# Four small probability-times-value units and a 32-row key matrix in a fused two-attention kernel

## The chip, the cores and the metric

One core of a Trainium2 chip. The time is that of one execution on the device, in microseconds (us). The median of three runs of the kernel before is 1574.19 us (1571.65 to 1574.8).

## What is computed

```python
# x (16, 100, 128), ctx_768 (16, 1444, 96): a Flamingo-like block, float32
x = x + tanh(g_xattn[0]) * xattn(layernorm(x), ctx_768, ...)     # 16 heads of 64, 1444 keys
x = x + tanh(g_ffn[0]) * ffn(layernorm(x), ...)
# ffn(X): per batch of 100 tokens, 16 heads of 8 (the "small attention"), then a mixture of 8 experts
h = rmsnorm(X, norm1_w)
q, k, v = (h @ wq), (h @ wk), (h @ wv)          # each (b, 100, 16, 8)
scores = einsum('bshd,bthd->bhst', q, k) / sqrt(8)
attn = softmax(scores)
ctx = einsum('bhst,bthd->bshd', attn, v)
X = X + ctx @ wo
...                                              # router, top 2 of 8 experts, shared expert
```

## The kernel before

Everything is written by hand, engine by engine, with semaphores. The main loop runs over the 16 batches; batch 0 ("first") and batch 15 ("last") are written out, and the other 14 are a hardware loop whose body holds an odd and an even batch. One turn here means one batch. The score matrix of the large attention (1444 keys x 1600 rows of head and token) is worked through in 24 units a batch: 12 chunks of the keys (eleven of 128 and one of 36) for each half of the heads. In unit i PE issues `score_unit` (L728 to L732: six products of 400 columns, f16 in high and low parts), then `pv_unit` for the unit two before (L747: again six products). ACT takes each unit's scores through two exponentials (L951, L952), and `probs_rest` (L431) makes the low half `p_lo`, on DVE or, for the units in `LO_POOL`, on POOL. PV products of unit i need the `p_lo` of unit i - 2. Chunk 11 of each half has 36 keys: its scores are 36 columns wide (unit 11), its PV products have 36 contraction rows (unit 13).

All else of a batch is cut into small aux units, which `plan` puts into the 24 units by hand; `steps` splits each unit's list in three: after the scores, between the first pair of PV products and the other four (`middle`), and at the end. Each aux unit writes one of two PSUM banks in turn, and PE waits before a unit until the one before the last is out of its bank (`last` in `run_aux`). The kinds: `t` and `q` transposes and query products for the next batch, `p` a product whose row maximum DVE takes (L813 on PE, L1247 on DVE; the planner spreads 39 of them by `LOAD` and `F_LOAD`, expected DVE loads), `y0`/`y1` the output of the large attention (L840, L1265, L1269), and `f`, the small attention of the batch before. Its units, in order, with the main unit i in which each is put:

- f0 (8) transposes the normalized tokens; f1 (9) makes q, k and v (L847 to L849). DVE copies `qT` and `v9` and builds `kbd` (L1276): the key matrix copied for all 16 heads, zero outside a head's 8 rows, 128 x 1600.
- f2 to f5 (10, 11, 12, 13) are the scores of four heads each: one product of `qT` with 400 columns of `kbd` over 128 rows (L853; an f32 product shows as two records). DVE takes the maxima and subtracts them (L1281, L1282), ACT the exponential (L961).
- f6 to f9 (12, 13, 14, 15) transpose the probabilities (L858); ACT copies them out to `pT` (L999).
- f10 (16) is probability times value, 16 heads in a row (L862: weights 100x100, 9 columns), and DVE divides (L1286, L1287). f11, f12 (18, 19) transpose and multiply by wo; f13 (23) is the transpose for the experts.

So with k the third of a unit: unit 14 has f8, one `p`, two `p`; unit 15 has `y0`, then f9 and a `p`, then two `p`; unit 16 `y0`, f10, `p`; unit 17 `y0`, a `p`, two `p`. Behind the last batch the same small attention runs once more among the first experts (`LAST`, with expert units `e` between). Three functions carry the order of PE: `run_aux`, `aux` and the loop body.

## Time and profile before

| | us |
|---|---|
| median of three runs | 1574.19 |
| span of the profiled execution, first to last instruction | 1570.3 |
| what lies around it, against that median | 3.9 |

The page's slices of the span, in 40 equal parts, digits in tenths; PEclk is the granted TensorE clock:

```profile
PE   5789999999999999999998999999999999888898
DVE  2787767766776767676766777667767685765765
PEclk9599999999999999999999999999999999899999
```

A view of the trace names an instruction by its line, engine, output and inputs, and the shape (partitions x elements). For PE, 97*128 is the contraction rows and the output rows of the product; x2 says that two records were merged. A duration of merged records is from the first start to the last end, and an end of PE is modelled, so starts are the safer reading. In brackets stands how long the engine sat idle before it, and what ended that.

### The profile page before, as it was taken

Reading aid. Unit: us, or ns where it says so; the run is one execution under the profiler, and the core shown is the slowest. Engines: PE = TensorE matmul, PEld = TensorE weight load, DVE = VectorE, ACT = ScalarE, POOL = GpSimd, SP = SyncE. Lnnn points to the kernel's source line nnn. Section 1 sums busy time; section 2 is a strip of 40 time slices with the busy share of each in tenths; the row PEclk is TensorE's granted clock in tenths of the full one; section 3 lists DMA queues with packets and bytes.
Section 4 is the critical chain, followed back from the end, with each engine's and each line's share of the span. In section 5 each row is a group of like instructions: output and inputs, shape, how many; then the busy total and the mean of one; then the engine's idle time right before and its main releaser. Section 6 shows DMA issues by size and latency. Waiting matters only on the chain.

```text
span 1570.3 us, 29033 instructions
## 1 busy us (share of the span) xinstructions
PE 1432.2 (91%) x8968; PEld 849.7 (54%) x8968; DVE 1085.7 (69%) x1948; ACT 832.3 (53%) x1236; POOL 561.2 (36%) x705
## 2 busy tenths in 40 slices
PE   5789999999999999999998999999999999888898
PEld 4245555555555555555555555555555645555676
DVE  2787767766776767676766777667767685765765
ACT  2145656565656555555545565656555554454554
POOL 3023333333333333243333343333333243444554
PEclk9599999999999999999999999999999999899999
DMA  7000000000000000000000000000000000000000
GB/s 195 0 15 1 15 1 16 1 17 1 15 1 16 1 5 11 2 16 1 15 1 16 1 15 1 16 1 15 1 13 4 1 1 1 1 1 1 7 7 11
DMA packets 14994, 18.08 MB, mean 12 GB/s; under 512 B 3046, under 2 KB 12490, under 8 KB 14858
## 3 DMA queue, kind: packets, MB, share of 16 engines
q1 hardware_dynamic: 14858, 16.26, 3.6%
q8 instruction: 86, 1.41, 0.4%
q14 instruction: 50, 0.41, 0.1%
HBM read 15.38 MB, written 0.82 MB: 10 GB/s over the span
## 4 chain that ended last, share of the span: by engine, by line
PE 59%; DVE 17%; issue 9%; ACT 6%; POOL 5%; DMA 1%; DVEq 1%; POOLq 0%; ACTq 0%; SPq 0%
PE psum L747 13%; PE psum L728 7%; PE psum L813 6%; PE psum L732 6%; PE psum L730 6%; DVE mx L1247 4%; PE psum L840 4%; PE psum L760 3%; PE psum L862 3%; ACT p_hi L952 3%; PE psum L853 3%; PE psum L773 2%; DVE p_lo L431 2%; DVE kbd L1276 2%; POOL p_lo L431 2%
## 5 line engine op out<-in xcount | busy, mean ns | idle before, releaser
L951 ACT ACTIVATE p<-psum 128x800 f32<-128x800 f32 (+1 forms) x384 | 321.3, 837 | 564.1 <-PE psum L732 558.2
L1247 DVE TENSOR_REDUCE mx<-psum 128x1 f32<-128x512 f32 (+3 forms) x624 | 387.2, 652 | 63.5 <-PE psum L813 58.5
L431 POOL TENSOR_TENSOR p_lo<-p,p_hi 128x800 f16<-128x800 f32 x128 | 236.3, 1847 | 472.9 <-ACT p_hi L952 461.2
L952 ACT ACTIVATE p_hi<-psum 128x800 f16<-128x800 f32 (+1 forms) x384 | 318.8, 830 | 0.0
L431 DVE TENSOR_TENSOR p_lo<-p,p_hi 128x800 f16<-128x800 f32 (+1 forms) x256 | 269.2, 1051 | 54.5 <-ACT p_hi L952 25.5
L813 PE MATMUL psum<-cT_hi,qk_hi 96*128 96x512 f16 (+3 forms) x624 | 236.2, 389 | 47.2 <-DVE mx L1247 15.0
L747 PE MATMUL psum<-p_hi,c_hi 128*128 128x400 f16 (+1 forms) x768 | 197.4, 338 | 21.3 <-POOL p_lo L431 14.7
L728 PE MATMUL psum<-qk_hi,cT_hi 97*128 97x400 f16 (+1 forms) x768 | 198.3, 340 | 11.7 <-ACT p_hi L952 5.5
L730 PE MATMUL psum<-qk_lo,cT_hi 96*128 96x400 f16 (+1 forms) x768 | 198.0, 339 | 0.0
L732 PE MATMUL psum<-qk_hi,cT_lo 96*128 96x400 f16 (+1 forms) x768 | 197.3, 339 | 0.0
L747 PE MATMUL psum<-p_lo,c_hi 128*128 128x400 f16 (+1 forms) x768 | 195.9, 336 | 0.0
L747 PE MATMUL psum<-p_hi,c_lo 128*128 128x400 f16 (+1 forms) x768 | 195.0, 336 | 0.0
L813 PEld LDWEIGHTS psum<-cT_hi,qk_hi 96*128 96x128 f16 (+1 forms) x624 | 61.2, 98 | 175.5 <-DVE mx L1247 71.9
L566 POOL TENSOR_TENSOR y_sum<-y_sum,y_sb 100x128 f32<-100x128 f32 x192 | 107.9, 562 | 55.3 <-DVE y_sb L1269 32.9
L556 POOL TENSOR_TENSOR c_lo<-ctx_nat,c_hi 128x1056 f16<-128x1056 f32 (+1 forms) x32 | 40.1, 1273 | 234.9 <-ACT c_hi L940 234.9
L747 PEld LDWEIGHTS psum<-p_hi,c_hi 128*128 128x128 f16 (+1 forms) x768 | 70.6, 100 | 80.2 <-issue 26.4
L730 PEld LDWEIGHTS psum<-qk_lo,cT_hi 96*128 96x128 f16 (+1 forms) x768 | 76.0, 99 | 58.5 <-issue 4.2
L732 PEld LDWEIGHTS psum<-qk_hi,cT_lo 96*128 96x128 f16 (+1 forms) x768 | 75.2, 98 | 59.4 <-issue 5.1
L747 PEld LDWEIGHTS psum<-p_hi,c_lo 128*128 128x128 f16 (+1 forms) x768 | 74.8, 97 | 57.5 <-issue 2.7
L728 PEld LDWEIGHTS psum<-qk_hi,cT_hi 97*128 97x128 f16 (+1 forms) x768 | 68.7, 99 | 63.6 <-issue 30.8
L747 PEld LDWEIGHTS psum<-p_lo,c_hi 128*128 128x128 f16 (+1 forms) x768 | 72.3, 101 | 50.6 <-issue 13.2
L621 POOL TENSOR_TENSOR p_lo<-p,p_hi 128x400 f16<-128x400 f32 x72 | 67.7, 945 | 73.6 <-ACT p_hi L966 73.3
(189 smaller groups left out, 1952.4 us busy)
## 6 DMA issues: line engine op xcount, KB each, us to landing
ctx_nat<-in_ctx_dram SPq DMA_DIRECT2D x16, 528.0 KB
wg<-in_L_ffn_e_gate_dram SPq DMA_DIRECT2D x1, 1024.0 KB, 5.5
wu<-in_L_ffn_e_up_dram SPq DMA_DIRECT2D x1, 1024.0 KB, 7.8
wd<-in_L_ffn_e_down_dram SPq DMA_DIRECT2D x8, 128.0 KB, 5.7
out_dram<-sqb SPq DMA_DIRECT2D x4, 200.0 KB
x<-in_x_dram SPq DMA_DIRECT2D x1, 600.0 KB
p<-in_L_xattn_w_q_dram SPq DMA_DIRECT2D x1, 512.0 KB, 4.2
wd_hi<-in_L_xattn_w_o_dram SPq DMA_DIRECT2D x1, 512.0 KB
```

The costliest lines, as they stand in the source:

```text
L431: engine.tensor_tensor(p_lo[0:m, i % 3, :, :], p32[0:m, i % 3, :, :], p_hi[0:m, i % 3, :, :], ALU.subtract).then_inc(lo_made(b, i)[0], 1)
L566: g.tensor_tensor(to, x, y, ALU.add).then_inc(y_add, 1)
L621: g.tensor_tensor(hid_lo[:, n % HS, :], hidden[:, n % 3, :], hid_hi[:, n % HS, :], ALU.subtract).then_inc(hid_lo_out, 1)
L728: mm(outs[k], cT_hi[parity][:, cols], qk_hi[parity][:, qs[k]], start=True, stop=False)
L730: mm(outs[k], cT_hi[parity][0:C, cols], qk_lo[parity][:, qs[k]], start=False, stop=False)
L732: t = mm(outs[k], cT_lo[parity][:, cols], qk_hi[parity][0:C, qs[k]], start=False, stop=True)
L747: t = mm(outs[k], w[parity][0:m, j, :], p[0:m, i % 3, k, :], start=(j == 0 and w is c_hi and p is p_hi), stop=(j == CH - 1 and w is c_lo))
L813: t = mm(bank[0:r, 0:w], qk_hi[parity][0:C, rt * P:rt * P + r], cT_hi[parity][0:C, part * MW:part * MW + w], start=True, stop=True)
L840: t = mm(bank[0:S, k * YW:(k + 1) * YW], acc_sb[half][:, h // 4, (h % 4) * S:(h % 4 + 1) * S], Nh[:, half * HALF + h, :], start=True, stop ...
L951: a(p32[0:m, i % 3, :, :], src, ACT.Exp, scale=DH ** -0.5)
L952: a(p_hi[0:m, i % 3, :, :], src, ACT.Exp, scale=DH ** -0.5).then_inc(probs_hi, 1)
L1247: v.tensor_reduce(mx[0:r, rt, part:part + 1], bank[0:r, 0:w], AX.X, ALU.max)\
```

## The change

The probability-times-value unit f10 becomes f10 to f13, of four heads each, in units 14, 15, 16 and 17; the later units move up by three numbers and keep their places. DVE divides for each quarter. The key matrix is built for four heads (128 x 400), by a mask that repeats every 32 rows, and each score unit multiplies the 32 rows of its four heads. POOL makes that mask in the setup with three small additions. The expected loads change, and with them the places of the `p` units: unit 9 gets two in place of one, unit 14 two in place of three, and all other counts stay. Thirds: unit 9 has f1, a `p`, a `p`; unit 14 has f8, f10, two `p`; unit 15 has `y0` and f9, then f11 and a `p`, then two `p`; unit 16 has f12 where f10 was; unit 17 has f13 and a `p` in the middle. Behind the last batch the four quarters follow each other.

```diff
     plan[8].append(("xf", 0))
-    for n, i in enumerate((8, 9, 10, 11, 12, 13, 12, 13, 14, 15, 16, 18, 19, 23)):
+    for n, i in enumerate((8, 9, 10, 11, 12, 13, 12, 13, 14, 15, 14, 15, 16, 17, 18, 19, 23)):
         plan[i].append(("f", n))
...
     NPU = RT * MP
-    F_LOAD = {0: .3, 1: 2.1, 6: 0, 7: 0, 8: 0, 9: 0, 10: .6, 11: .3, 12: .3, 13: .3}
+    F_LOAD = {0: .3, 1: 1.2, 6: 0, 7: 0, 8: 0, 9: 0, 10: .4, 11: .4, 12: .4, 13: .4, 14: .3, 15: .3, 16: .3}
     LOAD = {"t": .7, "q": .6, "y0": 0.55, "y1": 0.55, "ln": .5, "xf": .4, "rs": .5, "h2": .2}
...
     LAST = []
-    for n, unit in enumerate([("y1", 0), ("y1", 1), ("y1", 2), ("ln", 0), ("xf", 0)] + [("f", n) for n in range(13)] +
-                             [("rs", 0), ("h2", 0), ("f", 13), ("r", 1)]):
+    for n, unit in enumerate([("y1", 0), ("y1", 1), ("y1", 2), ("ln", 0), ("xf", 0)] + [("f", n) for n in range(16)] +
+                             [("rs", 0), ("h2", 0), ("f", 16), ("r", 1)]):
         LAST.append(unit)
-        at_most = {'y1': 1, 'ln': 4, 'xf': 0, 'rs': 2, 'h2': 0, 'r': 99, ('f', 2): 0, ('f', 3): 0, ('f', 4): 0, ('f', 5): 0, ('f', 10): 2}.get(unit if unit[0] == "f" else unit[0], 1)
+        at_most = {'y1': 1, 'ln': 4, 'xf': 0, 'rs': 2, 'h2': 0, 'r': 99, ('f', 2): 0, ('f', 3): 0, ('f', 4): 0, ('f', 5): 0, ('f', 10): 0, ('f', 11): 0, ('f', 12): 0, ('f', 13): 2}.get(unit if unit[0] == "f" else unit[0], 1)
         for _ in range(at_most):
...
 
-    F_STEPS = ["stats", "aggr", "xf", "h", "qT", "v", "mx0", "mx1", "mx2", "mx3", "rc",
+    F_STEPS = ["stats", "aggr", "xf", "h", "qT", "v", "mx0", "mx1", "mx2", "mx3", "rc0", "rc1", "rc2", "rc3",
                "stats2", "aggr2", "h2"]
...
         head_mask = sb("head_mask", [P, H])
+        mask4 = sb("mask4", [P, 4])
         minus_half = sb("minus_half", [P, H])
...
         qT = sb("qT", [D, S])
-        kbd = sb("kbd", [D, H, S])
+        kbd = sb("kbd", [D, 4, S])
         v9 = sb("v9", [S, H, DS + 1])
...
             step("head_mask", select(head_mask, DS - 1, [[DS, H]], -1, ALU.is_ge, 0.0))
+            step("mask 01", g.tensor_tensor(head_mask[:, 0:4], head_mask[:, 0:4], head_mask[:, 4:8], ALU.add))
+            step("mask 23", g.tensor_tensor(head_mask[:, 8:12], head_mask[:, 8:12], head_mask[:, 12:16], ALU.add))
+            step("mask4", g.tensor_tensor(mask4[:, :], head_mask[:, 0:4], head_mask[:, 8:12], ALU.add))
 
...
             set_wait(pe, set_act, SET_ACT, "Mh1")
-            set_wait(pe, set_pool, SET_POOL, "head_mask")
+            set_wait(pe, set_pool, SET_POOL, "mask4")
 
...
                         pe.wait_ge(aux_free, out_of(("f", 1)))
-                    t = mm(bank[0:S, 0:GW], qT[:, :], kbd[:, 4 * (n - 2):4 * (n - 1), :].rearrange("p a s -> p (a s)"),
+                    ds = slice(4 * DS * (n - 2), 4 * DS * (n - 1))
+                    t = mm(bank[0:S, 0:GW], qT[ds, :], kbd[ds, :, :].rearrange("p a s -> p (a s)"),
                            start=True, stop=True)
                 elif n < 10:
                     pe.wait_ge(exp_out, b * 4 + (n - 5))
                     for k in range(4):
                         t = tr(bank[0:S, k * S:(k + 1) * S], ex[:, n - 6, k, :], ident[0:S, 0:S])
-                elif n == 10:
-                    pe.wait_ge(pt_out, b * 4 + 4)
-                    for h in range(H):
-                        t = mm(bank[0:S, h * (DS + 1):(h + 1) * (DS + 1)], pT[:, h // 4, (h % 4) * S:(h % 4 + 1) * S],
-                               v9[:, h, :], start=True, stop=True)
-                elif n == 11:
-                    pe.wait_ge(aux_free, out_of(("f", 10)))
+                elif n < 14:
+                    pe.wait_ge(pt_out, b * 4 + (n - 9))
+                    for k in range(4):
+                        t = mm(bank[0:S, k * (DS + 1):(k + 1) * (DS + 1)], pT[:, n - 10, k * S:(k + 1) * S],
+                               v9[:, 4 * (n - 10) + k, :], start=True, stop=True)
+                elif n == 14:
+                    pe.wait_ge(aux_free, out_of(("f", 13)))
                     t = tr(bank[:, 0:S], sctx[:, :, :].rearrange("p h d -> p (h d)"), ident[0:S, 0:S])
-                elif n == 12:
-                    pe.wait_ge(aux_free, out_of(("f", 11)))
+                elif n == 15:
+                    pe.wait_ge(aux_free, out_of(("f", 14)))
                     t = mm(bank[0:S, 0:D], sctxT[:, :], sw[:, 3, :], start=True, stop=True)
...
 
-            set_wait(dve, set_pool, SET_POOL, "head_mask")
+            set_wait(dve, set_pool, SET_POOL, "mask4")
 
...
                     f_inc(cp(v9[:, :, 0:DS], bank[0:S, 2 * P:3 * P].rearrange("p (h d) -> p h d", d=DS)), b, "v")
-                    tt(kbd[:, :, :], bank[:, P:P + S].unsqueeze(1).broadcast_to([P, H, S]),
-                       head_mask[:, :].unsqueeze(2).broadcast_to([P, H, S]), ALU.mult).then_inc(aux_free, 1)
+                    tt(kbd[:, :, :], bank[:, P:P + S].unsqueeze(1).broadcast_to([P, 4, S]),
+                       mask4[:, :].unsqueeze(2).broadcast_to([P, 4, S]), ALU.mult).then_inc(aux_free, 1)
                 elif n < 6:
                     g = n - 2
                     sc = bank[0:S, 0:GW].rearrange("p (k s) -> p k s", s=S)
                     f_inc(v.tensor_reduce(mx4[:, g, :], sc, AX.X, ALU.max), b, f"mx{g}", True)
                     tt(ex[:, g, :, :], sc, mx4[:, g, :].unsqueeze(2).broadcast_to([S, 4, S]),
                        ALU.subtract).then_inc(aux_free, 1)
-                elif n == 10:
-                    o9 = bank[0:S, 0:H * (DS + 1)].rearrange("p (h d) -> p h d", d=DS + 1)
-                    f_inc(v.reciprocal(s_rc[:, :], o9[:, :, DS]), b, "rc", True)
-                    tt(sctx[:, :, :], o9[:, :, 0:DS], s_rc[:, :].unsqueeze(2).broadcast_to([S, H, DS]),
+                elif n < 14:
+                    hs = slice(4 * (n - 10), 4 * (n - 9))
+                    o9 = bank[0:S, 0:4 * (DS + 1)].rearrange("p (h d) -> p h d", d=DS + 1)
+                    f_inc(v.reciprocal(s_rc[:, hs], o9[:, :, DS]), b, f"rc{n - 10}", True)
+                    tt(sctx[:, hs, :], o9[:, :, 0:DS], s_rc[:, hs].unsqueeze(2).broadcast_to([S, 4, DS]),
                        ALU.mult).then_inc(aux_free, 1)
-                elif n == 11:
+                elif n == 14:
                     cp(sctxT[:, :], bank[:, 0:S]).then_inc(aux_free, 1)
-                elif n == 12:
+                elif n == 15:
                     tt(x2[:, bat(b), :].squeeze(1), bank[0:S, 0:D], xf[:, :], ALU.add).then_inc(aux_free, 1)
```

## Rows read from the trace of the kernel before

**Rows 1.** PE's and DVE's busy time on the page, with share of the span.

```profile
PE 1432.2 (91%) x8968; PEld 849.7 (54%) x8968; DVE 1085.7 (69%) x1948; ACT 832.3 (53%) x1236; POOL 561.2 (36%) x705
```

**Rows 2.** Windows of one turn: length, busy time by engine, PE clock, DMA.

```profile
240.50:324.00 83.50, 77.72 (x474) 45.08 (x472) 59.87 (x102) 47.43 (x68) 28.97 (x37) 1.00 0.03 8
324.00:406.90 82.90, 79.00 (x471) 46.03 (x472) 57.89 (x100) 46.13 (x67) 29.76 (x37) 0.98 0.03 8
...
490.60:571.90 81.30, 77.41 (x471) 45.17 (x472) 57.76 (x100) 46.11 (x67) 29.75 (x37) 1.00 0.03 8
571.90:658.20 86.30, 80.94 (x474) 46.73 (x473) 59.85 (x102) 47.51 (x68) 28.94 (x37) 0.96 0.02 8
...
741.00:828.10 87.10, 80.92 (x473) 46.77 (x471) 59.95 (x102) 47.52 (x68) 28.94 (x37) 0.96 0.03 8
...
1243.00:1328.40 85.40, 80.84 (x474) 46.96 (x473) 59.69 (x101) 46.83 (x68) 28.96 (x37) 0.96 0.00 1
```

**Rows 3.** Windows around falls of the clock, with the same columns.

```profile
618.50:621.90 3.40, 2.81 (x15) 1.32 (x16) 2.58 (x5) 2.33 (x4) 0.00 (x0) 1.00 0.00 0
621.90:625.30 3.40, 3.40 (x14) 1.93 (x12) 1.56 (x3) 1.98 (x4) 0.24 (x1) 0.50 0.00 0
...
632.20:635.60 3.40, 3.40 (x38) 3.18 (x37) 1.90 (x5) 0.98 (x2) 2.26 (x2) 1.00 0.02 5
635.60:639.00 3.40, 3.40 (x13) 1.95 (x12) 0.98 (x2) 0.34 (x1) 2.09 (x5) 0.50 0.00 0
...
802.80:809.60 6.80, 6.80 (x27) 4.05 (x27) 1.84 (x5) 1.57 (x2) 3.27 (x7) 0.50 0.00 0
```

**Rows 4.** Timeline of PE, unit 16 of the turn from 490.6.

```profile
549.26 2.91 PE L862 MATMUL psum<-v,pT 100*100 100x9 f32 x32
552.03 0.50 PE L747 MATMUL psum<-p_lo,c_hi 128*128 128x400 f16 x2
```

**Rows 5.** Timeline of PE, unit 14 of that turn.

```profile
542.67 0.57 PE L813 MATMUL psum<-cT_hi,qk_hi 96*128 96x512 f16 x2 [0.60 <-ACT pT L999]
```

**Rows 6.** Timeline of PE, unit 10 of that turn.

```profile
525.58 0.50 PE L747 MATMUL psum<-p_hi,c_hi 128*128 128x400 f16 x2
526.24 0.89 PE L853 MATMUL psum<-kbd,qT 128*100 128x400 f32 x2 [0.16 <-DVE kbd L1276]
```

**Rows 7.** Timeline of PE in batch 0, around products over 64 rows.

```profile
115.42 0.50 PE L747 MATMUL psum<-p_hi,c_lo 128*128 128x400 f16 x2
115.85 1.11 PE L826 MATMUL psum<-wd_hi,wd_lo 64*96 64x128 f32 x8
116.89 0.51 PE L728 MATMUL psum<-qk_hi,cT_hi 97*36 97x400 f16 x2
```

**Rows 8.** Timeline of PE, waits of unit 13, odd and even turn.

```profile
539.12 0.35 PE L813 MATMUL psum<-cT_hi,qk_hi 96*128 96x420 f16 x1 [0.28 <-ACT pT L999]
...
618.52 0.51 PE L747 MATMUL psum<-p_hi,c_hi 36*128 36x400 f16 x2 [0.39 <-DVE p_lo L431]
619.20 0.55 PE L858 MATMUL psum<-ident,ex 100*100 100x100 f32 x4 [0.16 <-DVE mx L1247]
...
621.25 0.35 PE L813 MATMUL psum<-cT_hi,qk_hi 96*128 96x420 f16 x1 [0.40 <-ACT pT L999]
```

**Rows 9.** Timeline of DVE, the low half of unit 11, odd and even turn.

```profile
534.59 0.97 DVE L431 TENSOR_TENSOR p_lo<-p,p_hi 36x800 f16<-36x800 f32 x1
...
615.97 2.50 DVE L431 TENSOR_TENSOR p_lo<-p,p_hi 36x800 f16<-36x800 f32 x1
```

**Rows 10.** Timeline of POOL, the low half of unit 12, the same turns.

```profile
534.60 2.53 POOL L431 TENSOR_TENSOR p_lo<-p,p_hi 128x800 f16<-128x800 f32 x1 [5.27 <-ACT p_hi L952]
...
615.92 1.71 POOL L431 TENSOR_TENSOR p_lo<-p,p_hi 128x800 f16<-128x800 f32 x1 [5.26 <-ACT p_hi L952]
```

**Rows 11.** Groups by line and shape: count, busy us, mean ns, idle before.

```profile
L1281 DVE TENSOR_REDUCE mx<-psum 100x4 f32<-100x400 f32 x64 | 36.4, 569 | 30.8 <-PE psum L853 30.8
...
L1276 DVE TENSOR_TENSOR kbd<-psum,head_mask 128x1600 f32<-128x1600 f32 x16 | 29.0, 1813 | 0.0
```

More of the change, by code:

```diff
@@ L191, in flamingo_kernel @@
                 "ones c_hi1", "pad c_lo1", "mx", "ones v9", "ones mask", "mask above", "head_mask",
-                "n1"] + [f"rank of {e}" for e in range(E)] + ["rw", "lnr1", "lnr2", "lnr3"]
+                "mask 01", "mask 23", "mask4", "n1"] + [f"rank of {e}" for e in range(E)] + ["rw", "lnr1", "lnr2", "lnr3"]
     LN_A, LN_B = ["sum", "mean", "centred"], ["square", "sumsq", "lnvar"]
```

## The prediction

> **What bounds the kernel now.** I read the page first: TensorE (PE) is busy 91% of the span and no other engine is above 69% [rows 1]. So time goes where PE's queue is longer or slower. The page's clock row shows full speed in almost every slice, which is too coarse. So second, the windows view with one window per turn of the batch loop: turns of one parity with the clock at 1.00 are equal (81.3 us where b is odd, 83.5 to 83.9 where it is even), and every longer one has a granted clock of 0.98 or 0.96 [rows 2] (six of the 14 turns stand there). Five odd turns have 0.98 and average 82.9: one period at the low level (0.50, which is 1.2 of 2.4 GHz) costs 82.9 - 81.3 = 1.6 us. The turn at 741.0 has 6.8 us at the low level and costs 87.1 - 83.7 = 3.4; the one at 1243.0 also has 6.8 us, and I price it the same, since it is the last of the loop and lacks the loop's return (some 1.5 us), which hides its loss. The turn at 571.9 has two separate periods and costs 2.6.
>
> Third, the same view around the falls. In that turn the clock is 0.50 from 635.6, right behind the block of 32 short matmuls of unit 16 (632.3 on), in which PE was busy 3.40 of 3.40 us [rows 3]. It also fell at 621.9, behind 618.5 to 621.9: PE busy 2.81 of 3.40, with the six products of the 36-row chunk in it [rows 3, 8]. Of the nine falls in the 14 turns eight stand behind L862's block, and one behind the 36-row stretch. PE was busy before each, so what counts is not only whether it is busy: streams of 9 columns, and streams through 36 rows, were followed by a slow clock. The eight cost 5 x 1.6 + 1.6 + 3.4 + 3.4 = 16.4 us, the ninth 2.6 - 1.6 = 1.0: 17.4 in all.
>
> **The change, part by part (PE time in one turn without a fall).**
>
> *The four quarters.* L862's 16 heads (32 records) take 552.03 - 549.26 = 2.77 us [rows 4]; a quarter takes 0.69. Unit 16 loses 2.08, units 15 and 17 gain 0.69 each. Unit 14 gains a quarter and loses one row-maximum product (0.22, which the planner moves to unit 9): +0.47. There PE waits 0.60 for ACT's copy of the transposed probabilities, which hangs on the exponentials and not on PE's extra work [rows 5], so the 0.47 goes into that wait: 0. Without that cover it would cost 0.47. Unit 9: +0.22. In unit 15 two aux units share the first third, and the two aux banks are used in turn; I add 0.1 for a wait on the copy. Sum: 0.69 + 0.69 - 2.08 + 0.22 + 0.1 = -0.38. DVE does four reciprocals and products in place of one pair: about 1 us more, beside PE; nothing else on its queue was last at those places.
>
> *The smaller key matrix.* L1276 takes 1.81 us on 128x1600; at 400 columns I take the 0.57 of L1281, a DVE instruction on 400 PSUM columns [rows 11]: 1.24 us less. PE's first score product waits for it: 526.24 instead of 525.58 + 0.34 = 525.92, so 0.32 comes back [rows 6]. Elsewhere DVE has idle time.
>
> *32 rows in place of 128.* Stream length is unchanged (400 columns), so I keep the 0.69 of a pair. But PE changes the part of the array it uses. No row shows 32 rows; the nearest is L826, 64 rows, in the first batch: L747 should end streaming at 115.42 + 0.34 = 115.76, L826 starts at 115.85, its eight take 1.04 until the next product at 116.89, where even spacing would give 0.87 [rows 7]. That is 0.09 to enter and 0.08 inside, 0.09 to leave: 0.17 in, 0.09 out. Bounds: 0 (were the queue to hide it, and less if a 32-row product were quicker) and twice that. I take the row. Score unit 0: -0.32 + 0.17 + 0.09 = -0.06. Score unit 1 already enters from a 36-column product: +0.09. Units 2 and 3 would pay 0.26 + 0.17 = 0.43.
>
> The Trainium skill, TensorEngine Tiling (Array Packing), section Tiling Modes, says that a change of tiling mode drains TensorE. The 0.09 us of rows 7 agrees with it; by the rule alone there would be no number.
>
> *A race behind it.* In unit 12 DVE and POOL come to their `p_lo` within 0.05 us of each other. At 534.59 DVE was first: DVE 0.97, POOL 2.53. At 615.97 POOL was: DVE 2.50, POOL 1.71 [rows 9, 10]. So odd turns have DVE first and even ones POOL, and PE idles 0.28 in unit 13 in the one and 0.39 + 0.16 + 0.40 = 0.95 in the other [rows 8]. DVE's start hangs on score unit 2; entering it 0.17 later puts POOL first in odd turns too: +0.67. In exchange the 0.43 is absorbed by that wait, in all turns. So this part gives: even -0.06 + 0.09 = +0.03, odd +0.70.
>
> With the quarters: even -0.35, odd +0.32; seven of each: -0.2 us. So without the clock the change is worth nothing; the time is decided by the clock.
>
> **The clock, old falls and new.** No quarter (0.69 us) holds as much short work as any block that preceded a fall, so I take back all 16.4 us. But units 10 to 13 now hold four products through 32 rows, where the only other fall stood behind products through 36. At present the stretch in unit 13 made the clock fall once in 14 turns; with 32-row products ahead of and inside it, and with the longer wait now in odd turns too, I take one turn in two: 7 falls (bounds: 1, as now, and 14). The length: the block that reached about 0.9 us into the slow period at 802.8 kept the clock low for 6.8 us, where others had 3.4 [rows 3]. Behind a fall in unit 13 the four quarters stand in units 14 to 17, and at the low level nothing there is quick. So I take half of the falls at two periods and half at three: 1.0 for the first (its cost in unit 13, where waits shrink) and 1.6 for each further: (2.6 + 4.2) / 2 = 3.4. 7 x 3.4 = 23.8, against the old 17.4: +6.4.
>
> **Ends.** The attention of the last batch is a serial chain; there the 1.24 us of L1276 count in full, the four quarters wait for each other's banks (+0.3), and its four score units stand nearly back to back, so I take one slow period for it (+1.6); in the last batch of the loop's form, where PE has less other work, +0.5. Sum +1.2. Three small POOL instructions in the setup lie in idle time: 0.
>
> Sum against the profiled span: 1570.3 - 0.2 + 6.4 + 1.2 = 1577.7; the median run is 3.9 us above that span, so 1581.6; I say 1581.5.
>
> **Rivals.**
>
> *A: new slow periods (above), 1581.5.* For it: the fall at 621.9 with PE busy. Against it: it is one fall, and the stretch also held waits. If all 14 turns fall: 24 us more, 1605. With four falls of two periods: 1568. A chance of 0.63, of which 0.45 is slower by over 0.2%, 0.11 within, 0.07 faster.
>
> *B: rows don't matter to the clock, 1560.* Then only today's ninth kind remains, in perhaps three turns, since its waits now stand in odd turns too: 3.0. The sum is -17.4 + 3.0 - 0.2 - 0.4 (ends without the slow period) = -15.0, so 1559.2; I say 1560. The point: if the clock in units 13 to 17 is 1.00 in more than four turns of five, the change is clearly faster. For it: products of 96 to 128 rows surround the 32-row ones, at full speed. Chance 0.27. The Trainium skill, TensorE: Matmul & The Clock Gate, Part 1, says that the gate follows how busy PE has been, and gives idle gaps as what lowers it. By that alone a 32-row product counts like any other, which is this rival; but rows 3 show a fall behind a stretch in which PE's records have no gap at all, so the rule as stated is not enough here.
>
> *C: the array's switching costs nothing.* Then odd turns keep DVE first, and each turn gains 0.32 + 0.38 = 0.70: -9.8 in place of -0.2, and with A's falls 1572. For it: PE loads weights ahead elsewhere. Against it: rows 7. Chance 0.10, half of it within 0.2%, half faster or slower with the falls.
>
> **How the numbers follow.** A measurement of this kernel can tell about 0.2% (3.1 us) from no change. Slower: 0.45 of A and 0.02 of C: 0.47. Within: 0.11 and 0.05: 0.16. Faster: 0.27 + 0.07 + 0.03 = 0.37. The range goes from B with 3 us below it (its falls gone), 1557, to A with 11 falls, 1595; beyond it lies a tenth at each end. The likeliest case alone: 1568 to 1595.
>
> **What would show it.** Windows of one turn each: PE clock under 1.00 in about seven turns, with the onset in unit 13 or 14 and not behind unit 16; L853 from `qT` in 32 rows with starts 0.09 us late; DVE's 36x800 `p_lo` near 2.5 us in every turn; PE's wait of 0.60 in unit 14 down to about 0.13; no PE wait on `kbd`. The forecast is wrong if the turns are at clock 1.00 (B), or if the low level lasts through units 14 to 17 in every turn, which would be well above the range.

## The result, and the profile after

The kernel after takes 1588.54 us (median of ten runs, 1579.87 to 1599.51), the kernel before 1573.99 us beside it (ten runs, 1567.74 to 1581.89). The ratio is 1.0102, with a 95% interval of 1.0075 to 1.0129: slower by 1%. I forecast 1581.5 and "slower" with a chance of 0.47. The profiled execution of after is the longest of its ten, at 1599.51 us, with a span of 1597.8 us; so its count of falls is likely above that of a median run, which I estimate below.

The page of after, engine totals and the clock slices:

```profile
PE 1462.8 (92%) x8968; PEld 855.4 (54%) x8968; DVE 1092.2 (68%) x2044; ACT 832.7 (52%) x1236; POOL 555.3 (35%) x708
...
PEclk9699999998989899998999899989999998899999
```

PE is busy 30.6 us longer than in [rows 1], with the same number of records. The clock row, all nines in the body of the loop before, now has an eight in every few slices. Windows of one turn each (length; busy time of PE, PEld, DVE, ACT, POOL; clock; DMA share and GB/s), to be read against [rows 2]:

```profile
153.50:236.00 82.50, 78.15 (x473) 44.71 (x471) 58.85 (x106) 46.74 (x68) 28.93 (x37) 1.00 0.03 8
497.50:584.30 86.80, 82.66 (x471) 47.18 (x472) 58.80 (x106) 46.07 (x67) 28.89 (x37) 0.94 0.02 8
755.30:839.10 83.80, 78.32 (x473) 44.67 (x471) 59.34 (x108) 47.46 (x68) 28.92 (x37) 1.00 0.03 8
```

An odd turn with the clock at 1.00 is 82.5 us; it was 81.3. An even one is 83.8 to 84.7 and was 83.5 to 83.9. A turn at 0.94, of which there was none before, is 86.8. A window just ahead of such a fall, one of the fall itself, and one of a short fall, with the columns of [rows 3]:

```profile
543.10:546.50 3.40, 3.17 (x15) 1.10 (x13) 2.74 (x4) 2.09 (x4) 0.24 (x1) 1.00 0.02 5
546.50:556.70 10.20, 9.77 (x38) 6.09 (x38) 3.75 (x7) 3.41 (x7) 1.70 (x1) 0.50 0.00 0
...
321.20:324.60 3.40, 3.40 (x14) 1.99 (x12) 0.98 (x1) 1.91 (x3) 0.00 (x0) 0.50 0.03 7
```

The clock stays at 0.50 (the 1.2 GHz level) for 10.2 us, three of the old 3.4 us periods in a row. The fourteen turns hold eight such falls, all of which begin in unit 13 or 14 (at 372.4, 457.8, 546.5, 717.2, 887.8, 1058.5, 1232.6 and 1317.9), and two of one period at the head of a turn. None stands behind unit 16, where eight of the nine old falls were. One long fall costs 86.8 - 82.5 = 4.3 us in an odd turn.

The two spans (1570.3 and 1597.8) differ by 27.5 us. By turns: the falls of the fourteen turns cost 8 x 4.25 + 3.3 = 37.3 against 17.4 before, +19.9. Turns without a fall are longer by 1.2 (odd) and about 0.45 (even), +11.6. What lies ahead of the second batch is 3.9 shorter, and the last batch 0.2.

For other runs I use this estimate: a kernel's profiled time less its profiled falls in the fourteen turns is its time without falls, and the median less that is what the falls cost in a median run. For after: 1599.5 - 37.3 = 1562.2, and 1588.5 - 1562.2 = 26 us, some six long falls and not eight. The estimate is good to some 4 us: the ten runs of e10 (below), whose profiled run has no fall in these turns, still spread from 1573.7 to 1581.7.

### The profile page after: what moved, and what is told of

It is laid out like the page before. It is cut to its first block, busy times and chain, and to the rows that moved or that the text cites. A ratio compares the mean times of both kernels' runs of the same rounds, so it can differ in the third digit from the quotient of the medians.

```text
span 1597.8 us, 29348 instructions
## 1 busy us (share of the span) xinstructions
PE 1462.8 (92%) x8968; PEld 855.4 (54%) x8968; DVE 1092.2 (68%) x2044; ACT 832.7 (52%) x1236; POOL 555.3 (35%) x708
## 4 chain that ended last, share of the span: by engine, by line
PE 56%; DVE 16%; issue 12%; POOL 6%; ACT 6%; DMA 1%; DVEq 1%; POOLq 1%; SPq 0%; ACTq 0%
PE psum L751 13%; PE psum L732 7%; PE psum L817 6%; PE psum L736 6%; PE psum L734 6%; DVE mx L1252 5%; PE psum L764 3%; ACT p_hi L957 3%; PE psum L844 3%; DVE p_lo L432 3%; PE psum L777 2%; PE psum L858 2%; POOL p_lo L432 2%; PE psum L867 2%; DVE y_sb L1274 2%
## 5 line engine op out<-in xcount | busy, mean ns | idle before, releaser
L432 POOL TENSOR_TENSOR p_lo<-p,p_hi 128x800 f16<-128x800 f32 x128 | 229.9, 1796 | 520.7 <-ACT p_hi L957 510.6
L432 DVE TENSOR_TENSOR p_lo<-p,p_hi 128x800 f16<-128x800 f32 (+1 forms) x256 | 280.1, 1094 | 52.4 <-ACT p_hi L957 23.0
L817 PE MATMUL psum<-cT_hi,qk_hi 96*128 96x512 f16 (+3 forms) x624 | 240.3, 394 | 45.8 <-DVE y_sb L1274 20.5
L751 PE MATMUL psum<-p_hi,c_hi 128*128 128x400 f16 (+1 forms) x768 | 198.7, 340 | 19.0 <-POOL p_lo L432 15.6
L751 PEld LDWEIGHTS psum<-p_hi,c_hi 128*128 128x128 f16 (+1 forms) x768 | 68.7, 100 | 81.7 <-issue 27.3
```

Of the source, the lines that this page charges most:

```text
L432: engine.tensor_tensor(p_lo[0:m, i % 3, :, :], p32[0:m, i % 3, :, :], p_hi[0:m, i % 3, :, :], ALU.subtract).then_inc(lo_made(b, i)[0], 1)
L751: t = mm(outs[k], w[parity][0:m, j, :], p[0:m, i % 3, k, :], start=(j == 0 and w is c_hi and p is p_hi), stop=(j == CH - 1 and w is c_lo))
L817: t = mm(bank[0:r, 0:w], qk_hi[parity][0:C, rt * P:rt * P + r], cT_hi[parity][0:C, part * MW:part * MW + w], start=True, stop=True)
```

## The experiments

Twelve kernels ran, each timed beside the kernel before (1569.5 to 1573.3 us). Theory R: the clock falls because the four score products now run through few contraction rows. Rivals: the four quarters that stand behind them, the new waits, and later the stops at both ends of a 32-row product, which the texts below call the change of the array's division. e3, e4, e9 and e11 add heads that don't belong together, so their scores are not the reference's; all other kernels compute what the reference computes.

| run | us | ratio to before (95%) | falls of the clock in the 14 turns of the profiled run |
|---|---|---|---|
| after | 1588.5 | 1.0102 (1.0075-1.0129) | 8 of three periods, 2 of one |
| e1_rows_only | 1592.4 | 1.0102 (1.0060-1.0144) | 10 from unit 13/14 (half of one period, half of two), 10 behind unit 16 |
| e2_split_only | 1571.0 | 0.9976 (0.9950-1.0003) | none |
| e3_rows_128 | 1550.3 | 0.9841 (0.9801-0.9881) | none |
| e4_rows_64 | 1588.4 | 1.0097 (1.0069-1.0125) | 3 of three |
| e5_ysb3 | 1589.4 | 1.0089 (1.0054-1.0124) | 7 of three, 3 of one |
| e6_split_placed | 1562.3 | 0.9933 (0.9908-0.9958) | none |
| e7_q_masked | 1554.6 | 0.9870 (0.9844-0.9896) | none |
| e8_q_masked_ysb3 | 1544.9 | 0.9818 (0.9792-0.9843) | none |
| e9_rows_68 | 1558.9 | 0.9931 (0.9895-0.9967) | 3 of one |
| e10_switch_full_rows | 1577.1 | 1.0026 (1.0003-1.0050) | none |
| e11_rows_68_switch | 1590.1 | 1.0108 (1.0070-1.0146) | 3 of three, 3 of one |
| e12_masked_no_split | 1563.5 | 0.9956 (0.9930-0.9982) | 7 behind unit 16, 1 in unit 14 |

### Each half of the change alone

e1_rows_only is the kernel before with the 32-row keys, their mask and their building as in after; its probability-times-value unit stays whole.

```diff
-        kbd = sb("kbd", [D, H, S])
+        kbd = sb("kbd", [D, 4, S])
...
-                    t = mm(bank[0:S, 0:GW], qT[:, :], kbd[:, 4 * (n - 2):4 * (n - 1), :].rearrange("p a s -> p (a s)"),
+                    ds = slice(4 * DS * (n - 2), 4 * DS * (n - 1))
+                    t = mm(bank[0:S, 0:GW], qT[ds, :], kbd[ds, :, :].rearrange("p a s -> p (a s)"),
```

> The kernel before with the key matrix for four heads and 32 rows only; the probability-times-value unit stays whole. Theory R (few rows let the clock fall): new slow periods begin in unit 13 in about half of the 14 turns, mostly one period long since no quarters follow in units 14 and 15, beside some 8 behind the whole block of unit 16; odd turns are longer by 0.8 us because POOL now takes its low half first; 1580 to 1592. Rival Q (the quarters make the clock fall, rows don't matter): clock in unit 13 as before, one turn in 14, and only the 0.8 us in odd turns: 1576 to 1580.

e2_split_only is the kernel after with the key matrix and the score product of before.

```diff
-                    ds = slice(4 * DS * (n - 2), 4 * DS * (n - 1))
-                    t = mm(bank[0:S, 0:GW], qT[ds, :], kbd[ds, :, :].rearrange("p a s -> p (a s)"),
+                    t = mm(bank[0:S, 0:GW], qT[:, :], kbd[:, 4 * (n - 2):4 * (n - 1), :].rearrange("p a s -> p (a s)"),
```

> The changed kernel with the key matrix for 16 heads and 128 rows as before: the split alone. Theory R: at most four slow periods in the 14 turns, all from unit 13; per turn the units 9 and 14 to 17 cost 0.4 us more than before (the changed kernel's wait of 0.66 us for y_sb in unit 17 is still there); 1563 to 1571. Rival Q: slow periods of three in a row in half of the turns stay: 1583 or more.

Measured: 1592.4, just above R's range, with more falls and longer ones than R had, and 1571.0, within it. The keys alone bring the whole loss, with falls from unit 13 or 14 in ten turns; the split alone takes away every fall of the fourteen turns. So the new falls are not the quarters' doing, and the old ones behind the block are gone with it. The quarters do bear on the length: without them the falls of e1 from unit 13 or 14 last one or two periods, and then the clock is back at 1.00 until the next one, behind unit 16, where all eight of after last three. One turn of e1:

```profile
546.00:552.80 6.80, 6.57 (x21) 3.17 (x22) 2.89 (x5) 3.33 (x6) 1.68 (x1) 0.50 0.00 0
552.80:563.10 10.30, 10.03 (x80) 7.56 (x79) 6.17 (x13) 3.52 (x5) 2.87 (x4) 1.00 0.00 0
563.10:566.50 3.40, 3.40 (x13) 2.04 (x12) 1.10 (x3) 1.57 (x2) 1.60 (x5) 0.50 0.02 5
```

Yet the split alone gains little, because its turns without a fall are longer (odd 82.7 for 81.3). Part of that is a wait that is neither in before nor in after. PE, then DVE, in unit 9 of e2_split_only:

```profile
525.39 0.39 PE L817 MATMUL psum<-cT_hi,qk_hi 96*128 96x512 f16 x1 [1.09 <-DVE kbd L1280]
...
523.53 1.81 DVE L1280 TENSOR_TENSOR kbd<-psum,head_mask 128x1600 f32<-128x1600 f32 x1
```

The planner now puts two row-maximum products into unit 9, and the second stands behind DVE's 1.81 us on the large key matrix. With the small one (0.565 us in every batch of after) it has no wait. e6_split_placed moves one of the two to unit 8 by giving aux unit 1 the load of before:

```diff
-    F_LOAD = {0: .3, 1: 1.2,
+    F_LOAD = {0: .3, 1: 2.1,
```

> The split alone (16-head key matrix, 128 rows), with the load of f1 as in the kernel before, so that unit 9 holds one row-maximum product and unit 8 two. Theory: the wait of 1.09 us on the key matrix in unit 9 goes (15 us over the turns), no new slow period: 1553 to 1561. Rival (PE meets the key matrix later at f2 instead): only some 10 us, 1560 to 1564.

Measured: 1562.3, above the theory's 1553 to 1561 and in the rival's range; odd turns 82.1, still no fall. The rival was right in its mechanism too: against e2, unit 9 is 1.44 us shorter, but unit 8 is 0.57 longer and unit 10 0.33, where the first score product now meets the key matrix. The 0.43% between the ratios of e2 and e6 is the price of one expected load in the planner's table.

### Rows

e3_rows_128 and e4_rows_64 change one line of the kernel after: which rows the score product covers. First e3, then e4:

```diff
-                    ds = slice(4 * DS * (n - 2), 4 * DS * (n - 1))
+                    ds = slice(0, P)
```

```diff
-                    ds = slice(4 * DS * (n - 2), 4 * DS * (n - 1))
+                    ds = slice(64 * ((n - 2) // 2), 64 * ((n - 2) // 2) + 64)
```

> The changed kernel, but each score product runs over all 128 rows of the small key matrix (it adds the heads of all four groups, so the small attention's scores are not the reference's); nothing else differs, no instruction more or less. Theory R: the slow periods in units 13 to 17 go, as in the split alone, and the switching of the array and the late start of DVE's low half with them: 1560 to 1569. Rival Q, or a rival by which the smaller key matrix itself (DVE ahead by 1.2 us) sets off the falls: they stay, 1583 or more.

> As the one with 128 rows, but over 64 rows (two groups of heads are added, so the scores are not the reference's). Theory R: the fall depends on how many rows stream, so its number lies between those of 32 and of 128 rows: two to six turns with slow periods; the cost of switching the array stays as with 32 rows (starts 0.09 us late, 0.17 us longer per unit): 1570 to 1582. Rival: switching itself lets the clock fall, whatever the rows: as with 32 rows, 1583 or more.

Measured: 1550.3, below the whole range that I had written, and 1588.4, above it. Two windows of one turn each, e3_rows_128, even and odd:

```profile
430.50:513.70 83.20, 77.51 (x473) 45.22 (x472) 57.71 (x108) 46.80 (x67) 29.71 (x37) 1.00 0.03 8
513.70:595.10 81.40, 77.32 (x473) 45.28 (x472) 57.71 (x108) 46.79 (x67) 29.70 (x37) 1.00 0.03 8
```

With 128 rows no turn has a fall, with 64 rows the loss of a median run is that of 32 (20 us of falls by the estimate above: 1588.4 less 1581.9 - 13.1). Against after, an odd turn without a fall also loses 1.1 us. The timelines of PE at a score product show a part of it, first after, then e3_rows_128:

```profile
790.50 0.50 PE L751 MATMUL psum<-p_hi,c_hi 128*128 128x400 f16 x2
790.93 0.91 PE L858 MATMUL psum<-kbd,qT 32*100 32x400 f32 x2
791.77 0.51 PE L751 MATMUL psum<-p_lo,c_hi 128*128 128x400 f16 x2
```

```profile
521.09 0.50 PE L751 MATMUL psum<-p_hi,c_hi 128*128 128x400 f16 x2
521.43 0.83 PE L858 MATMUL psum<-kbd,qT 128*100 128x400 f32 x2
522.10 0.50 PE L751 MATMUL psum<-p_lo,c_hi 128*128 128x400 f16 x2
```

Entering the 32-row product takes 790.93 - (790.50 + 0.34) = 0.09 us and the product to its successor 0.84; over 128 rows it is 0.00 and 0.67. Together 0.26 us, my two terms of 0.17 and 0.09.

But e3 and e4 differ in two things: a 64-row or 32-row product has few rows, and it has these stops at its ends. Three more runs take the two apart.

### Few rows, or the stops?

e9_rows_68 takes rows 0 to 67: hardly more than 64, but its trace shows no stop (unit 10 takes 3.02 us, as over 128 rows, and 3.29 in after).

```diff
-                    ds = slice(4 * DS * (n - 2), 4 * DS * (n - 1))
+                    ds = slice(0, 68)
```

> The kernel after with the small score product of each unit taken over rows 0 to 67 of the small key matrix and of q (the scores add the heads of the groups that lie in those rows, so they are not the reference's); nothing else changes. It feeds about as few contraction rows as the 64-row run, but it is no product of 32 or 64 rows, so that the array need not be divided for it. Theory R (few rows in the products of units 10 to 13 let the clock fall): three-period falls in unit 13 or 14 as with 64 rows, in three or more of fourteen turns, while the entry and exit of the score product cost what they do over 128 rows; 1570 to 1588 us. Rival S (it is the change of the array's division, or the stop that goes with it, that lets the clock fall): no fall in a loop turn, odd turns 81.4 us as over 128 rows, 1549 to 1557 us.

e10_switch_full_rows has 128 rows (it is e7_q_masked, below) and a tiny product ahead of each score product that has the stops.

```diff
+                    mm(bank[0:S, 0:8], qT[0:32, n - 2, :], kbd[0:32, 0, 0:8], start=True, stop=True)
                     t = mm(bank[0:S, 0:GW], qT[:, n - 2, :], kbd[:, :, :].rearrange("p a s -> p (a s)"),
```

> The kernel with the small key matrix and masked copies of q over 128 rows, with one tiny product of 32 rows and 8 columns set ahead of each unit's score product (the score product overwrites its result). It has the change of division in each of the four units and all 128 rows in the long products. Theory R (few rows): no fall in a loop turn; the time is that of the masked kernel, 1554.6, and 56 products more at 0.2 to 0.45 us each on a path that TensorE bounds, 1560 to 1580 us, with a granted clock of 1.00 in every turn. Rival S (the change of division): three-period falls from unit 13 or 14 in five or more turns as after, 1580 us or more.

e11_rows_68_switch has both: the 68 rows of e9 and the tiny product.

> The 68-row run (whose scores add heads, so are not the reference's) with the tiny product of 32 rows and 8 columns set ahead of each unit's score product: few rows and the change of the array's division together, where each of the two has been run without the other (three one-period falls in fourteen turns with few rows, none with the change of division). Theory RS (the falls need both: few rows, and the stops of a change of division that thin the stream further): three-period falls in units 13 and 14 in three or more of fourteen turns, 1580 to 1592 us. Theory R (the count of the rows that the product itself uses decides, by degrees, and the change of division adds only its time): few falls, of one period, as with 68 rows, 1575 to 1583 us, the 68-row time and 56 x 0.43.

Measured: 1558.9, 1577.1, 1590.1. The view that decides is the stretch of units 10 to 13 in a window of its own, in one odd turn without a fall of e3_rows_128, e9_rows_68, e10_switch_full_rows and e11_rows_68_switch, in this order:

```profile
190.58:205.03 14.45, 13.98 (x71) 6.91 (x70) 10.15 (x17) 9.46 (x15) 4.23 (x2) 1.00 0.01 2
```

```profile
187.53:201.98 14.45, 13.98 (x71) 6.90 (x70) 10.16 (x17) 9.45 (x15) 4.22 (x2) 1.00 0.01 2
```

```profile
190.24:206.28 16.04, 15.57 (x80) 7.66 (x79) 11.29 (x17) 9.46 (x15) 3.40 (x2) 1.00 0.01 2
```

```profile
190.37:206.40 16.03, 15.56 (x80) 7.65 (x78) 11.28 (x17) 9.46 (x15) 3.40 (x2) 1.00 0.01 2
```

These are two twin pairs. Within a pair the length and the busy time of every engine agree to 0.02 us, and the numbers of records are the same but for one weight load; e3 and e9 differ in nothing but the rows of four products, e10 and e11 beside these in DVE's write of q, which e10 makes in four masked copies ahead of the stretch's products. With 128 rows neither twin has a fall in fourteen turns. With 68 rows both have: three of one period without the stops (two of them in unit 14, one at the head of a turn), three of three periods and three of one with them. The times say the same: the four runs of e3 lie from 1548.7 to 1552.1 us, the seven of e9 from 1550.9 to 1565.0, and the intervals of the ratios to before don't overlap within either pair. The twins of a pair ran on different chips, but e9 and e10 on the same one, and there too only 68 rows bring falls. One fall of each, from e9_rows_68 and from e11_rows_68_switch:

```profile
532.60:536.00 3.40, 3.40 (x15) 2.13 (x13) 1.66 (x3) 1.50 (x3) 0.00 (x0) 0.50 0.00 0
```

```profile
548.70:558.90 10.20, 9.92 (x38) 6.10 (x38) 3.75 (x7) 3.41 (x7) 1.70 (x1) 0.50 0.00 0
```

So the stops alone leave the clock at full speed, few rows alone let it fall, and with both together some falls last three periods. By the estimate, the falls of a median run cost 0 us in e10 (1577.1 in both), 12 in e9 (1558.9 - (1550.9 - 4.6)), 21 in e11 (1590.1 - (1587.9 - 18.6)), 20 in e4 and 26 in after. For e10, R's forecast held and the rival's fell. For e9 both missed: R wanted long falls and 1570 us or more, the rival none. For e11 the forecast of "both" held, in falls and time; only its word that the falls need both is too strong, since 68 rows alone have short ones. So, as far as these runs go, rows decide whether there are falls, and the stops add to them. That they make them longer is seen in one profiled run each, and less surely: the profiled run of e9 is the fastest of its seven, the others are 5.7 to 14.1 us longer, and how long the falls are in those isn't known.

The pairs also shut out two rivals, and the other runs a third. The long wait behind the `p_lo` race is in none of the four (e11 has PE waiting 0.32 us in unit 13, as e10), so it isn't needed for the falls. And PE's share of busy time is the same in both twins, so no account of it as the profile measures it tells them apart. Nor is it the values of the scores: with the reference's scores the clock falls in after and not in e10, with others it falls in e9 and not in e3.

### A new wait that the change brings

e5_ysb3 is the kernel after with a third `y_sb` buffer.

```diff
-        y_sb = sb("y_sb", [S, 2, 3, D])
+        y_sb = sb("y_sb", [S, 3, 3, D])
...
-                y = y_sb[:, (half * len(YB) + n) % 2, :, :]
+                y = y_sb[:, n, :, :]
```

> The changed kernel with three y_sb buffers in place of two, so that DVE's third division of a half needn't wait for POOL's sums of the first. Theory: PE's wait of 0.66 us in unit 17 (on y_sb, behind POOL's low half of unit 16) goes in every turn, 9 us of PE time; the falls of the clock stay as they are or change a little with the shorter stretch: 1572 to 1587. Rival (the wait in unit 17 comes from DVE's own queue, four small divisions more): it stays, and the time is that of the changed kernel, 1580 to 1597.

The reason for it stands in units 16 and 17 of after, on PE, DVE and POOL:

```profile
819.18 0.79 PE L867 MATMUL psum<-v,pT 100*100 100x9 f32 x8
820.63 0.39 PE L817 MATMUL psum<-cT_hi,qk_hi 96*128 96x512 f16 x1 [0.66 <-DVE y_sb L1274]
...
820.15 0.42 DVE L1274 TENSOR_TENSOR y_sb<-psum,y_rc 100x256 f32<-100x256 f32 x1 [0.85 <-POOL y_sum L570]
...
816.89 2.13 POOL L432 TENSOR_TENSOR p_lo<-p,p_hi 128x800 f16<-128x800 f32 x1 [7.12 <-ACT p_hi L957]
818.98 0.45 POOL L570 TENSOR_TENSOR y_sum<-y_sb 100x128 f32<-100x128 f32 x1
819.58 3.43 POOL L570 TENSOR_TENSOR y_sum<-y_sum,y_sb 100x128 f32<-100x128 f32 x6
```

Read it from the bottom. POOL's `p_lo` of unit 16 runs until 819.0, and only then do its sums read the `y_sb` buffers. DVE's next scaling needs one of the two, waits 0.85 us for the sum, and PE waits 0.66 us for DVE. Unit 16 used to be 2.1 us longer on PE, and in that time POOL was through. The waits views of after and then of e5_ysb3 give it over the whole run (us in total, times, longest):

```profile
PE psum L817 <- DVE y_sb L1274: 20.5, 30, 1.5
...
PE psum L817 <- ACT pT L1004: 5.8, 18, 0.4
```

```profile
PE psum L817 <- DVE y_sb L1274: 10.4, 16, 1.2
```

The third buffer takes the wait away, and unit 17 goes from 4.65 to 4.01 us. In odd turns 0.36 us of it comes back in unit 11 (3.97 for 3.61), where PE now waits for DVE:

```profile
364.50 0.39 PE L817 MATMUL psum<-cT_hi,qk_hi 96*128 96x512 f16 x1 [0.41 <-DVE ex L1287]
```

So the fourteen turns save some 6.5 us on PE. The median is 1589.4, against my expected 1572 to 1587; the two ratios differ by 0.0013 with intervals of 0.0027 and 0.0035 to each side, so a saving of 6.5 us (0.4%) is neither shown nor ruled out. If it is missing, the clock is where it went: by the estimate above (seven long falls and three short in the profiled run, 34 us) the falls cost 34 us in a median run of e5 and 26 in after. With full rows the same edit is worth 0.5% (e8, below); of the 10.2 us between the spans of e7 and e8 the fourteen turns have 6.6, and most of the rest lies ahead of them.

### Without the few rows

e7_q_masked keeps the small key matrix and the right scores, but runs over 128 rows: DVE writes four copies of q, each with the rows of the other groups at zero.

```diff
-                    f_inc(cp(qT[:, :], bank[:, 0:S]), b, "qT")
+                    f_inc(tt(qT[:, :, :], bank[:, 0:S].unsqueeze(1).broadcast_to([P, 4, S]),
+                             gmask[:, :].unsqueeze(2).broadcast_to([P, 4, S]), ALU.mult), b, "qT")
...
-                    t = mm(bank[0:S, 0:GW], qT[ds, :], kbd[ds, :, :].rearrange("p a s -> p (a s)"),
+                    t = mm(bank[0:S, 0:GW], qT[:, n - 2, :], kbd[:, :, :].rearrange("p a s -> p (a s)"),
```

> The changed kernel, with the small key matrix of four heads, but the queries as four masked copies (zero outside a group's 32 rows), so that each score product runs over 128 rows and the result is the reference's. DVE pays some 0.3 us more per turn for the copies. Theory R (the number of rows streamed counts, zeros or not): no slow period in the 14 turns, as with the summed heads: 1548 to 1556. Rival (rows of zeros don't count as work): slow periods in units 13 to 16 as with 32 rows, 1580 or more.

e8_q_masked_ysb3 adds the third `y_sb` buffer of e5.

> Masked queries over 128 rows and three y_sb buffers together. Theory: the parts add: the wait of 0.66 us in unit 17 and the falls are both gone: 1538 to 1548. Rival (the shorter stretch of units 14 to 17 lets the clock fall again, or another wait takes the place): 1549 or more.

e12_masked_no_split puts these keys into the kernel before, its unit of 32 short products whole.

> The kernel before with the small key matrix and masked copies of q over 128 rows, and the probability-times-value unit left whole: the other part of the masked kernel alone. If the whole block's eviction-free stretch is what lets the clock fall there (theory: the falls behind unit 16 belong to the block and not to the keys), its falls behind unit 16 stay at about eight in fourteen turns, 2.05 us each, and the time is that of before less 1 to 6 us for the cheaper key matrix, 1566 to 1574 us. Rival: with the small key matrix the shares of the turn shift enough for the falls to go, 1554 to 1562 us, and the split brings nothing of its own.

Measured: 1554.6, 1544.9 and 1563.5. The first two are inside what was expected. The third lies between the two ranges: its falls are those of the first theory, and so are the 6.0 us below its own before, but that before was itself only 1569.5. In e7 three quarters of the rows carry zeros of q and the clock doesn't fall. What counts is thus the rows that a product runs through, not the values in them. An odd turn of e7:

```profile
487.00:568.70 81.70, 77.44 (x471) 45.24 (x472) 57.80 (x106) 46.13 (x67) 29.78 (x37) 1.00 0.03 8
```

The four copies of q have a price: unit 9 takes 3.40 us for the 3.09 of e3, 0.3 us a turn.

e12 has its seven falls behind unit 16, so the old falls belong to the block and the split is what removes them: from 0.9956 to 0.9870, some 13 us. A turn of e8_q_masked_ysb3, the fastest kernel of this study, and a fall of e12_masked_no_split behind unit 16:

```profile
574.60:656.10 81.50, 76.90 (x469) 44.96 (x470) 57.45 (x106) 45.79 (x66) 30.22 (x37) 1.00 0.03 9
```

```profile
797.20:804.00 6.80, 6.80 (x26) 3.96 (x26) 1.96 (x6) 1.56 (x2) 3.28 (x7) 0.50 0.00 0
```

e8 computes what the reference computes, at 0.9818 of before (0.9792 to 0.9843): each of the two ideas of the change is worth having, once the keys are kept at 128 rows.

## Why the prediction was right and where it failed

The likeliest case, new slow periods in units 13 to 17 for old ones behind unit 16, is what happened, and the time lies in the range, 7.0 us above the forecast. By its steps:

- **The old falls go with the block.** Right. None is left behind unit 16 in after, nor in any run with the quarters; e12, which keeps the block, has seven.
- **The new falls come from the 32-row products.** Right, and shown by the twins. The forecast said seven, from unit 13 or 14, at 3.4 us each, 23.8 in all. The profiled run has eight at 4.25 and two short ones, the median run about 26 us. My bound on the length was the mis-sized term: half at two periods and half at three, where in the profiled run of after all eight had three. For a median run the two misses, fewer long falls and longer ones, about cancel.
- **Rows don't matter to the clock (B), the rival at 1560.** Fallen, by e3 against after and by the twins.
- **Switching costs 0.17 in and 0.09 out.** Right in size, 0.26 together, and unit 10 shows it in full: 3.29 us in after, 3.02 in e3. Rival C, that it costs nothing, falls with it. But I let the wait in unit 13 absorb two of the four in all turns. In even turns it did, nearly (unit 12 +0.17, unit 13 -0.14); in odd turns the 0.17 of unit 12 (3.43 to 3.60) stayed on top of the race's price.
- **The race.** Right. DVE's and POOL's `p_lo`, in an odd and in an even turn of after:

```profile
541.79 2.39 DVE L432 TENSOR_TENSOR p_lo<-p,p_hi 36x800 f16<-36x800 f32 x1
...
799.61 2.38 DVE L432 TENSOR_TENSOR p_lo<-p,p_hi 36x800 f16<-36x800 f32 x1
...
541.63 1.70 POOL L432 TENSOR_TENSOR p_lo<-p,p_hi 128x800 f16<-128x800 f32 x1 [5.20 <-ACT p_hi L957]
...
799.45 1.70 POOL L432 TENSOR_TENSOR p_lo<-p,p_hi 128x800 f16<-128x800 f32 x1 [5.20 <-ACT p_hi L957]
```

POOL is first in both, where [rows 9, 10] had DVE first in odd turns, and odd unit 13 grew from 4.35 to 5.03 us, +0.68 for +0.67.

- **The key matrix.** Right: `kbd` takes 0.565 us for the 0.57 assumed, and no PE wait on it is left.
- **The quarters.** Three of four places as forecast: unit 16 -2.12 (-2.08), unit 9 +0.22, and unit 14 the same 3.77 us, its wait on ACT down from the 0.60 of [rows 5]:

```profile
206.64 0.57 PE L817 MATMUL psum<-cT_hi,qk_hi 96*128 96x512 f16 x2 [0.17 <-ACT pT L1004]
```

Unit 15 took +0.89 for 0.79, and unit 17 +1.39 for 0.69. **This last is the step that failed**: I took 2.08 us out of unit 16 and asked only who waits in the units that gain work. I didn't ask whose work the 2.08 us had covered. It was POOL's `p_lo` and the sums behind it, and 0.66 us of the gain came back one unit later as a wait, 14 x 0.66 = 9 us, more than the 7.0 us by which the forecast was low.
- **The sum without falls.** Forecast -0.2 us for the fourteen turns, measured +11.6, so 11.8 more: 9.8 of it is unit 17, nearly all of that the wait, 1.4 is unit 15, and 1.2 is unit 12 in odd turns. Units 10, 11 and 16 took some 0.1 us a turn less than forecast, and the rest lies mostly in the loop's return in unit 23, which varies by nearly 1 us from turn to turn.
- **Ends.** Forecast +1.2, measured about -4, nearly all of it ahead of the second batch. Half of that stands in the setup, which has nine low periods in a row for ten (from 41 us on); e12 has ten of them and nearly as short a setup, so the one needn't be the reason for the other. The other half stands in the first batch, which has its two low periods in a row where before had them apart, and the other runs fall into the same two kinds (84.4 to 86.2 us in a row, 87.1 to 87.3 apart). No edit goes with the kinds, so I take it for chance.

The last two misses have opposite signs and partly cancel, so the forecast is closer than its working; that is luck.

Open: why a fall behind few rows begins in unit 13 or 14 and not earlier, and why after has it in six odd turns of seven and in two even ones. Why it then lasts three periods is open in part: e1 shows that it needs the quarters, or something that came with them, while e5 and e11, which have quarters, stops and few rows, also have falls of one period. Open too are the one-period falls at the head of a turn: there are five, in after, e5, e9 and e11, none in a kernel with full rows, and all stand far behind the last few-row product, each right after one of its run's longest returns of the loop (unit 23 of 4.1 to 4.5 us). e3 and e10 have returns as long (4.34 and 4.45) and no such fall.

## What to carry to other kernels

When work is moved away from a place, ask what the moved time covered there on the slower engines, and look for the buffer whose reader stands behind it: what is freed comes back one unit later if that buffer is only two deep. In this kernel a product through a quarter of the contraction rows wasn't cheaper than one through all of them with the same columns: it cost 0.26 us more and, through the clock, some 26 us in a median run, 1.6% of the kernel. Zeros in the unused rows kept the clock up, for 0.3 us a turn to write them. And a saving on a TensorE that bounds the kernel has to be read together with the granted clock of the same turns: e5 took 0.64 us off every unit 17, and the median didn't move beyond its noise.

## What the hardware showed that I had not expected

- Rows of zeros keep the clock up: e7 runs at 1.00 in all fourteen turns with three of four rows of q at zero, and after, which leaves these rows out, has 10.2 us at 1.2 GHz in eight of them.
- The twins e10 and e11 agree in PE's busy time to 0.01 of 15.6 us over the stretch ahead of the falls, and only the one with 68 rows has falls. PE's busy time in the profile doesn't say what the clock goes by.
- A tiny product of 32 rows and 8 columns between full ones costs about 0.44 us: units 10 and 12 grow from 3.02 and 3.43 (e7) to 3.46 and 3.87 us (e10). Some of it is hidden in unit 11; the four add 1.6 us to an odd turn (81.7 to 83.3).
